# The expert outputs of a step: both heads in a row, or one behind each half of the next step's hidden units

## The reference

```python
h = x @ Wm + bm
t = h.reshape(bs * L_ * H, HD)
logits = t @ expert_emb
w = jax.nn.softmax(logits, axis=-1)
topw, topi = jax.lax.top_k(w, K)
hmid = jax.nn.gelu(jnp.einsum('td,edi->tei', t, W1) + b1, approximate=False)
eo = jnp.einsum('tei,eio->teo', hmid, W2) + b2
sel = jnp.take_along_axis(eo, topi[:, :, None], axis=1)
comb = (sel * topw[:, :, None]).sum(axis=1)
out = comb.reshape(bs, L_, d)
return out @ Wo + bo
```

## Time and profile before

| | us |
|---|---|
| median of 3 runs | 452.73 (452.68 to 453.31) |
| the profiled execution, its own time | 453.17 |
| its span, first to last instruction | 451.4 |
| PE busy | 371.9 (82% of the span) |
| DVE busy | 297.3 (66%) |
| ACT busy | 241.8 (54%) |
| POOL busy | 105.6 (23%) |

### The profile page before, as it was taken

The page is one execution under the profiler, slowest core; times in us unless marked ns, Lnnn a source line. Parts: engine busy times, 40 slices in busy tenths (PEclk is TensorE's granted clock), DMA queues, the critical chain, the costliest instruction groups (busy, mean ns, idle before and its releaser), DMA issues.

```text
span 451.4 us, 7262 instructions
## 1 busy us (share of the span) xinstructions
PE 371.9 (82%) x2684; PEld 163.9 (36%) x2684; DVE 297.3 (66%) x596; ACT 241.8 (54%) x291; POOL 105.6 (23%) x149
## 2 busy tenths in 40 slices
PE   0641988988888897999988979999879799969995
PEld 0520323434324453443353534433535322213112
DVE  7373887565886878778757787777468655943332
ACT  1120002592003498686553886865547888758970
POOL 8009100026001420244333202443230023222000
PEclk9995555999556999999998999999999999989999
DMA  8014000024000054455110444552005055803540
GB/s 294 13 29 101 12 1 2 3 61 78 5 2 5 0 91 52 123 138 162 24 27 1 82 60 117 135 144 54 25 2 71 10 143 158 126 8 112 166 121 23
DMA packets 26847, 31.43 MB, mean 70 GB/s; under 512 B 6454, under 2 KB 17718, under 8 KB 26678
## 3 DMA queue, kind: packets, MB, share of 16 engines
q1 hardware_dynamic: 23740, 28.84, 27.1%
q0 software_dynamic: 3072, 2.13, 2.7%
HBM read 3.47 MB, written 1.05 MB: 10 GB/s over the span
## 4 chain that ended last, share of the span: by engine, by line
PE 57%; DVE 18%; ACT 12%; issue 8%; DMA 2%; POOL 1%; SPq 1%; ACTq 0%; DVEq 0%; POOLq 0%
PE misc L1055 21%; PE big L1055 17%; PE acc L1055 16%; ACT ring L600 9%; DVE mx L838 7%; PE misc L1074 2%; ACT qk_turned L608 2%; DVE xn L784 2%; SPq L328 1%; ACT L633 1%; DMA q_block<-qk_turned 1%; DVE stats L759 1%; DMA gm<-wT 1%; DVE sil L717 1%; POOL gm L545 1%
## 5 line engine op out<-in xcount | busy, mean ns | idle before, releaser
L600 ACT ACTIVATE ring<-big 128x1024 f32<-128x1024 f32 (+1 forms) x224 | 197.1, 932 | 158.3 <-PE big L1055 156.6
L838 DVE TENSOR_REDUCE mx<-misc 128x1 f32<-128x512 f32 (+7 forms) x176 | 100.4, 591 | 33.5 <-PE misc L1055 30.1
L1055 PE MATMUL misc<-k_dense,q_block 128*128 128x512 bf16 (+7 forms) x256 | 79.6, 375 | 23.7 <-DMA q_block<-qk_turned 14.4
L1055 PE MATMUL acc<-ring,cb 128*32 128x512 f32 x512 | 69.2, 616 | 5.4 <-ACT ring L600 4.4
L1055 PEld LDWEIGHTS misc<-k_dense,q_block 128*128 128x128 bf16 x256 | 31.3, 150 | 87.7 <-DVE mx L838 63.2
L1055 PE MATMUL big<-tstack,w1s 128*128 128x512 bf16 x192 | 55.5, 381 | 8.5 <-ACT ring L600 7.0
L1055 PE MATMUL big<-q_dense,k_block 128*128 128x512 bf16 (+7 forms) x256 | 55.5, 322 | 4.7 <-ACT ring L600 3.8
L961 DVE SCALAR_TENSOR_TENSOR gm<-acc,cb,gm 128x512 f32<-128x512 f32 x40 | 29.9, 747 | 27.6 <-DMA gm<-wT 14.4
L1055 PEld LDWEIGHTS big<-q_dense,k_block 128*128 128x128 bf16 x256 | 30.7, 148 | 33.2 <-ACT ring L600 21.0
L1055 PE MATMUL misc<-later_key,identb 128*128 128x64 bf16 (+2 forms) x176 | 42.5, 242 | 0.0
L1055 PE MATMUL acc<-ring,vals 128*32 128x64 f32 (+7 forms) x512 | 40.9, 424 | 0.5
(11 more groups left out here) (148 smaller groups left out, 411.9 us busy)
## 6 DMA issues: line engine op xcount, KB each, us to landing
gm<-wT SPq DMA_DIRECT2D x64, 256.0 KB
tstack<-tp SPq DMA_DIRECT2D x18, 128.0 KB, 5.1
k_dense<-qk SPq DMA_DIRECT2D x24, 64.0 KB
k_block<-qk_turned POOLq DMA_DIRECT2D x48, 32.0 KB, 3.5
q_dense<-qk SPq DMA_DIRECT2D x24, 64.0 KB
ca<-in_pack_a SPq DMA_DIRECT2D x1, 1155.0 KB, 5.2
xs<-in_x SPq DMA_DIRECT2D x4, 256.0 KB, 7.9
q_block<-qk_turned SPq DMA_DIRECT2D x32, 32.0 KB
```

What stands on the lines that cost most here:

```text
L600: act.activation(dst, src, func, scale=scale).then_inc(s["ring_read"], 1)
L838: dve.tensor_reduce(mx[:, g, k:k + n, blk], src, AX.X, ALU.max).then_inc(s["misc_read"], 1)
L1055: return pe.matmul(dst, lhsT, rhs, start=start, stop=stop)
```

## The change

PE's order alone is changed. The outputs of both heads of a step are issued where so far those of head 0 stood: behind the first two hidden units of the next step. Behind hidden units 2 and 3 no outputs follow. The numbers of instructions, their sizes, and the orders of all other engines stay as they are; no DMA is moved.

```diff
+            def outputs_of_step(b, phase, sums_read, step):
+                for k in range(2):
+                    outputs(b, phase, sums_read, step, k)
+
             def combine(here, k):
...
                     maxima(here, units[1:2])
-                    if t >= 3:
-                        outputs(b, phase, sums_read, step - 1, k)
+                    if t >= 3 and k == 0:
+                        outputs_of_step(b, phase, sums_read, step - 1)
                     maxima(here, units[2:])
...
                     if t == 2 and begun:
-                        outputs(b, phase, sums_read, 0, 0)
+                        outputs_of_step(b, phase, sums_read, 0)
                     elif t == 2:
                         routed(here)
...
-                        outputs(b, phase, sums_read, 0, 0)
+                        outputs_of_step(b, phase, sums_read, 0)
                     if t in between:
                         between[t]()
```

## The result

The changed kernel takes 469.76 us (median of 6 runs, 469.15 to 472.72) where the kernel before, run beside it, takes 453.67 (6 runs, 452.68 to 457.75): a ratio of 1.0352, interval 1.0302 to 1.0402. It is slower, by 16 us. The forecast was 467.2 us, in a range of 458 to 472. The profiled execution took 470.29 us with a span of 468.5; before, 453.17 and 451.4. Ratios compare fast runs alone; of the profiles, that of the run with DVE's slots later is of a slow execution (462.74 us), whose two loop turns stand at a granted clock of 1.00 and 0.99.

A forecast was written before the change was run, and what follows sets the result against it. PE mostly bounds (57% of the chain), tied with ACT in the last turn. Loops 5.8 + late turn 2.7 + last turn 6.0 = 14.5 us on 453.17 gave 467.7; median 0.44 lower, 467.2 us, range 458 to 472.

The forecast's parts named there:

- The last turn: Final turn, PE and ACT tied: ACT idles behind each pair, steps 5.02 for 4.17 us, seven pairs, +6.0 us.
- the one with the combination: Step containing the combination, same shape as outputs: in the last turn slips more beside it; in loops free, DVE catching up.
- the same lags: Delays read from the old last turn: hidden unit to Gelu 0.65, to outputs 0.55, Gelu to Gelu 0.92, PE resuming 0.04.
- The loop's turns: Two loop turns: DVE holds PE, six steps each at +0.48, so +2.9 a turn, +5.8 us for two.
- The chain to the sixth unit: Loop step: from outputs through DVE's work until PE may write the sixth unit of the maxima, 4.17 us; step 5.75.
- the place of the slot: Loop step: DVE takes the even slot, 0.55, before starting the fourth unit of the maxima, delaying the bank for the sixth.
- The late turn: Turn before the last: ACT's lags, then the tokens behind two groups, shift its last outputs by +2.7 us.
- the 1.8: Late turn: token matmul behind two groups delays DVE's split and the slot PE waits for; that pair comes 1.8 us late.
- The added wait: Second outputs group waits for the bank ACT empties after the step's last Gelu; first group covers it, otherwise up to 0.5 a step.
- the third rival: TensorE's granted clock falls with the last turn's new waits: pairs 3.7 us, about 19 us on top, 486; chance 0.04.
- the first rival: DVE does not hold PE in the loops: they give -2.6, the whole +6.1, 458.8 us; chance 0.20.
- PE's own saving: Every pair: two output groups in a row take PE 1.84 us instead of 2.00, saving 0.16 a pair.

The follow-up runs named there:

- the run with the last turn alone: Against the kernel before, both heads' outputs stand in a row only in the last turn, old order elsewhere: 460.24 against 454.49 us, ratio 1.0114.
- the five executions of the table: Profiled executions of the kernel before, the whole change, and the change in the last, loop or late turns only; ratios of those three 1.0114, 1.0161, 1.0078.

## Why the prediction was right, and where it was off

**The last turn: right.** The step was put at 5.02 and is 5.03, the turn at +6.0 and is +6.01, alone and in the whole. The first step and the one with the combination, which the prediction set apart, cost 0.85 and 0.86 like the others. The run with the third buffer shows that the reason holds too: 4.47 worked out from the same lags, 4.49 measured. That each pair costs the same wherever it stands, the rival of the run with the last turn alone, is out.

**The loop's turns: the mechanism right, two steps of eight missing.** The example step was put at 5.75 and takes 5.79. Step by step, from the pairs of after (183.62, 188.87, 194.66, 200.26, 206.47, 212.39, 219.84, 225.12, and the Exp at 231.36) against the groups of head 0 of before (182.72, 187.91, 193.16, 198.31, 203.98, 209.29, 216.48, 221.38, and the Exp at 227.23), the steps are longer by 0.06, 0.54, 0.45, 0.54, 0.61, 0.26 and 0.38, the last by 0.39. The six that the prediction charged give 2.91, as it said: +2.9. The two that it took for free, the first and the one with the combination, cost 0.32: that is what is missing to 3.23. In the step with the combination DVE does not catch up as was thought: it stands empty for 1.07 ahead of that step's third reduction (at 214.73), where before it was 0.21 (at 210.76). What makes the 0.26 of that step was not tried. That the next Exp waits for the scores holds for after, where ACT idles 2.05 ahead of 231.36; before, ACT came to it straight from its table load, at 227.23.

One sentence of it fails as a general one: that ACT's idling costs nothing there. It was nearly true of the change as made, as the run with halved Gelus alone shows (0.2 to 0.3 us), but only because DVE stood in front: behind DVE, ACT's chain was worth a further 1.05 us a turn. The chain to the sixth unit is in the trace term by term (1.85 + 0.48 + 0.55 + 0.65 + 0.67 = 4.20, for 4.17). But the place of the slot, on which the argument leaned, gives back only 1.0 to 1.2 of the 3.2 us a turn; with the slot out of the way the rest of DVE's work behind the pair holds PE, at 5.52 a step.

**The late turn: the size right, and the cause of the 1.8 too.** From its first outputs the pairs of after stand -0.01, 0.10, 0.96, 0.96, 1.83, 2.68 and 2.68 us later than head 0's groups of before. The prediction had 1.8 for the fifth of these, 2.7 for the sixth and the last. It put the 1.8 down to the token matmul and DVE's split, with PE waiting for DVE's slot, and so it is: the tokens come 1.83 later (389.83, and 379.94 before, from the first outputs of each), the slot ends 1.83 later, and the pair follows 0.15 behind it in both. What the prediction did not say is that ACT's chain, late by 1.0 since the third step as it had it, stands close behind: without the tokens' delay the pair would still be late, by 1.2 in the run with the tokens first, which pays for its own edit, and by some 0.85 by the estimate above. So the tokens' delay alone is worth 0.6 in that run, and up to 1.0 by the estimate; no run parts the two more closely.

The remaining 0.34 of the +3.02 arises behind the last outputs, where after has 11.89 and before 11.55 for the same instructions; the same stretch took 10.2 to 11.9 in the other runs. Nearly all of it is in that pair itself, up to the next matmul, after and then before (columns as above):

```profile
408.91:412.49 3.58, 3.58 (x17) 0.61 (x17) 0.75 (x1) 0.53 (x1) 1.27 (x1) 0.50 0.00 0
```

```profile
398.17:401.43 3.26, 3.26 (x16) 0.55 (x17) 1.99 (x4) 0.53 (x1) 1.59 (x1) 0.56 0.00 0
```

The granted clock is 0.50 (1.2 GHz) after 4.35 of waiting, and 0.56 after 3.77 before. The 0.32 by which the pair is longer is nearly the whole 0.34.

**The added wait and the rivals.** The pairs take 1.85 to 1.86 up to the next matmul in the steps read, so the second group's new wait costs nothing there. The clock of the last turn stays at 1.00 though ACT idles 1.26 in each step, so the third rival is out there. What it feared, a pair at 1.2 GHz for 3.7, stands at the end of the late turn alone (3.58, at 408.91), and before had nearly the same (3.26). The whole does not fall to 458.8, the first rival's time. The prediction's resolution was too fine: it took 0.9 us, 0.2%, as enough to tell from no change, and the interval of the ratio is 0.5% to either side.

**PE's own saving is real, and worth nothing here.** The pair takes 1.85 (188.87 to 190.72) where two lone groups take 2.00; PE's busy time in the first loop turn falls from 43.19 (same cut of the trace before) to 42.35. The Trainium skill, TensorEngine Tiling (Array Packing), Key Properties, says that changing the tiling mode drains TensorE. The trace agrees in sign with a gain from fewer changes, 0.15 us a pair; that the drain makes it was not tried. Only where work of DVE and ACT was left out did a loop turn with pairs come below the 44.51 of before, at 44.32.

**What the sum left out.** The forecast for the profiled execution was 467.7, and it took 470.29, 2.6 more: 0.66 from the loop's two turns, 0.32 from the late turn, 0.01 from the last, and 1.61 from stages that the change does not touch.

## What to carry to other kernels

Before merging two pieces of work on the busiest engine, ask how long every engine that it feeds can live on what is buffered: here two buffers hold 1.94 us of Gelus, and the first Gelu behind a pair can start only 3.18 behind the start of those two. A lone group of 1.00 left ACT idle for 0.27 a step and DVE for 0.74 at 189.38; the pair of 1.84 made it 1.26 and 1.60. Where a wait repeats in each step, follow it round until it closes on itself, and add it up (1.85 + 0.48 + 2.30 + 0.74 + 0.15 = 5.52): its terms say what can shorten the step. Changing the consumer's order took one term out of the chain (5.79 to 5.52), and then another chain took over. When one engine is relieved, look at once for the next limit, as a second one can stand 0.3 us a step behind the first. And when a view puts a wait for several semaphores down to one engine, compare the ends of all that the code waits for: at 394.93 the name was wrong.

## What the runs showed of the hardware that was not expected

The granted clock differs between executions in stretches where the instructions are the same, and moves the time of a stage by up to 2.6 us. The same stretch near the start, after and then before:

```profile
22.00:30.00 8.00, 6.68 (x39) 3.50 (x37) 4.07 (x6) 0.00 (x0) 0.00 (x0) 0.61 0.00 1
```

```profile
22.00:30.00 8.00, 5.94 (x39) 3.07 (x37) 4.40 (x7) 0.00 (x0) 0.00 (x0) 1.00 0.00 1
```

And two stretches of attention: after, in the stage between the second turn and the late turn (1.00 in that stage before), and before, in the stage between the two loop turns (1.00 in that stage after):

```profile
342.00:349.00 7.00, 6.78 (x61) 3.74 (x58) 2.07 (x4) 4.07 (x6) 0.00 (x0) 0.76 0.00 0
```

```profile
241.50:247.00 5.50, 5.50 (x32) 2.24 (x31) 4.08 (x10) 1.02 (x1) 1.48 (x2) 0.69 0.01 3
```

A mean of 0.6 to 0.8 is part of the stretch at 1.2 and part at 2.4 GHz. Over the five executions of the table the time of a stage follows its granted clock: between the loop turns 44.97 and 45.02 us at 1.00, 46.51 at 0.96, 47.52 and 47.53 at 0.93; before the late turn 40.60 twice at 1.00, 41.92 at 0.96, 42.74 and 42.84 at 0.92. What decides it in a given execution stays open: no run here was made for it. It means that of the 17.1 us between the two spans 1.6 say nothing of the change, and that a part of a few tenths of a us is better read from the pitch of steps at clock 1.00 than from the total.
